# Residual add of a mixing block: beta added to x on GpSimd, scale and add in one VectorE step

## What is computed

```python
# 0: gated mixing over time
ctx    = ema(x);  gated = x * sigmoid([x, ctx] @ Wg.T + bg)
mod    = 0.5 + sigmoid(gelu(x @ Wn1.T + bn1) @ Wn2.T + bn2)          # 16 rows
temporal = sum_d softmax(blend)[d] * ema_d(gated * mod[d])           # 16 traces
out = (gelu(x @ Wsoma.T + bsoma) * sigmoid(temporal @ Wtemp.T + btemp)) @ Wout.T
x   = x + (out - mean(out)) / sqrt(var(out) + 1e-5) * gamma + beta
# 1: masked attention pooling
score = tanh(x @ W1 + b1) @ v;  x = x + softmax(masked score) @ x / count
# 2: 8 experts and a shared one, 256 -> 1024 -> 256
x = x + (1 - sg) * sum_e g[e] * (silu(x@Wg[e]) * (x@Wu[e])) @ Wd[e] + sg * shared(x)
# 3: head, 256 -> 1024 -> 256, part of W2 chosen per sequence
x = x + gelu(x @ W1 + b1) @ [W2, We[idx]] + [b2, be[idx]]
```

## Time and profile before

| | |
|---|---|
| median of 3 runs | 2799.22 us (2799.05 to 2800.12) |
| profiled execution | 2799.28 us |
| its span, first to last instruction | 2797.3 us |
| TensorE busy | 2765.7 us, 12786 matmuls |
| VectorE, ScalarE, GpSimd busy | 1796.6, 1456.9, 1219.6 us |
| granted TensorE clock | 0.999 of full |
| DMA | 232.48 MB, 83 GB/s |

### The profile page before, as it was taken

The page is one execution under the profiler, slowest core; times in us unless marked ns, Lnnn a source line. Parts: engine busy times, 40 slices in busy tenths (PEclk is TensorE's granted clock), DMA queues, the critical chain, the costliest instruction groups (busy, mean ns, idle before and its releaser), DMA issues.

```text
span 2797.3 us, 36734 instructions
## 1 busy us (share of the span) xinstructions
PE 2765.7 (99%) x12786; PEld 2294.8 (82%) x12786; DVE 1796.6 (64%) x2975; ACT 1456.9 (52%) x2649; POOL 1219.6 (44%) x954
## 2 busy tenths in 40 slices
PE   8899999999999999999999999999999999999999
PEld 5678888888878888888888888888888888888888
DVE  8899778767877666557755766555765563333443
ACT  4655656565447544555545644444644563333445
POOL 6266336533554355334543345433454333333334
PEclk9999999999999999999999999999999999999999
DMA  5344334433223222122321232211332131111221
GB/s 179 110 138 123 98 108 115 133 93 108 81 59 109 93 68 68 55 61 76 97 65 57 85 92 74 62 53 57 108 82 62 44 100 46 46 46 46 79 90 58
DMA packets 119607, 232.48 MB, mean 83 GB/s; under 512 B 13816, under 2 KB 61184, under 8 KB 119424
## 3 DMA queue, kind: packets, MB, share of 16 engines
q1 hardware_dynamic: 84144, 192.27, 22.4%
q10 hardware_dynamic: 32688, 29.47, 4.2%
q0 software_dynamic: 2592, 8.41, 0.9%
HBM read 221.98 MB, written 8.11 MB: 82 GB/s over the span
## 4 chain that ended last, share of the span: by engine, by line
PE 93%; DVE 5%; issue 1%; ACT 1%; DMA 0%; POOL 0%; DVEq 0%; SPq 0%; ACTq 0%
PE bank L625 20%; PE bank L626 20%; PE bank L627 20%; PE ps_out L625 10%; PE ps_out L627 10%; PE ps_out L626 10%; PE bank L618 1%; DVE trace L1263 1%; DVE trace L1349 1%; DVE w_lo L1474 1%; DVE hid L1509 0%; DVE trace L1423 0%; PE bank L660 0%; PE bank L646 0%; PE bank L651 0%
## 5 line engine op out<-in xcount | busy, mean ns | idle before, releaser
L1655 POOL TENSOR_TENSOR hid_lo<-hid,hid_hi 128x512 fp32r<-128x512 f32 x640 | 850.5, 1329 | 1528.2 <-ACT hid_hi L1192 1527.9
L625 PE MATMUL bank<-res_lo,w_hi 128*128 128x512 f32 x2428 | 955.1, 393 | 5.2 <-DVE hid L1509 4.3
L626 PE MATMUL bank<-res_hi,w_lo 128*128 128x512 f32 x2428 | 946.2, 390 | 0.0
L627 PE MATMUL bank<-res_hi,w_hi 128*128 128x512 f32 x2428 | 945.2, 389 | 0.0
L1509 DVE TENSOR_TENSOR hid<-hid,bank 128x512 f32<-128x512 f32 x576 | 394.2, 684 | 619.5 <-PE bank L627 592.0
L1161 ACT ACTIVATE hid<-bank 128x512 f32<-128x512 f32 x576 | 343.9, 597 | 586.7 <-PE bank L627 583.8
L1474 DVE TENSOR_TENSOR w_lo<-w_raw,w_hi 128x768 fp32r<-128x768 f32 (+2 forms) x520 | 497.6, 959 | 191.0 <-ACT w_hi L1122 148.9
L1122 ACT ACTIVATE w_hi<-w_raw 128x768 fp32r<-128x768 f32 x392 | 331.3, 845 | 480.7 <-PE ps_out L627 468.6
L625 PEld LDWEIGHTS bank<-res_lo,w_hi 128*128 128x128 f32 x2428 | 456.2, 188 | 98.0 <-DVE w_lo L1474 4.7
L627 PEld LDWEIGHTS bank<-res_hi,w_hi 128*128 128x128 f32 x2428 | 455.8, 188 | 96.8
L626 PEld LDWEIGHTS bank<-res_hi,w_lo 128*128 128x128 f32 x2428 | 456.2, 188 | 89.2
(11 more groups left out here) (226 smaller groups left out, 1599.7 us busy)
## 6 DMA issues: line engine op xcount, KB each, us to landing
w_raw<-in_chunks SPq DMA_DIRECT2D x392, 384.0 KB, 3.1
mod_on<-mod_rows ACTq DMA_DIRECT2D x154, 128.0 KB, 3.2
w_raw<-in_head_chunks SPq DMA_DIRECT2D x64, 224.0 KB, 2.5
stat<-mod_rows ACTq DMA_DIRECT2D x70, 128.0 KB, 3.1
x_in<-in_xT SPq DMA_DIRECT2D x16, 256.0 KB, 3.7
pre_x<-in_xT SPq DMA_DIRECT2D x14, 256.0 KB, 7.0
soma_rows<-pre_soma SPq DMA_DIRECT2D x14, 256.0 KB, 2.0
soma<-soma_rows SPq DMA_DIRECT2D x14, 256.0 KB, 3.5
```

The lines of the kernel that those rows point to most:

```text
L625: mm(out, wh, xl, start=start and i == 0, stop=False, skip_group_check=not lone)
L626: mm(out, wl, xh, start=False, stop=False, skip_group_check=not lone)
L627: last = mm(out, wh, xh, start=False, stop=end, skip_group_check=not lone)
L1655: nc.gpsimd.tensor_tensor(hid_lo[i % DEPTH][:], hid[i % 3][:], f(hid_hi[i % DEPTH][:]), ALU.subtract).then_inc(s_hlo, 1)
```

## The change

For blocks 1 to 7 piece 36 takes the form of block 0: GpSimd adds beta to x in place ahead of the seventh add (j = 15), and VectorE forms `x1` in two SCALAR_TENSOR_TENSOR, after a wait for GpSimd's stage "xb". The stage "affine" is gone, and the price of piece 36 in the planner goes from 1.4 to 1.0.

```diff
-    return {0: 1.3, 5: 1.0, 34: 1.7, 36: 1.4, 42: 1.5, 24: 0.0, 25: 0.0, 29: 0.0, 37: 0.0, 43: 0.0}.get(j, 0.7)
+    return {0: 1.3, 5: 1.0, 34: 1.7, 36: 1.0, 42: 1.5, 24: 0.0, 25: 0.0, 29: 0.0, 37: 0.0, 43: 0.0}.get(j, 0.7)
...
-            + ["t_lo", "prod", "p_lo", "q_lo", "rstd", "norm", "affine", "x1", "score",
+            + ["t_lo", "prod", "p_lo", "q_lo", "rstd", "norm", "x1", "score",
...
-SIDE_POOL = ((ADDED[:6] + ["xb"] + ADDED[6:], ADDED[:6] + ["xb"] + ADDED[6:-1]), ADDED)
+SIDE_POOL = ((ADDED[:6] + ["xb"] + ADDED[6:], ADDED[:6] + ["xb"] + ADDED[6:-1]), ADDED[:6] + ["xb"] + ADDED[6:])
...
                 elif j == 36:
+                    dve.wait_ge(l_pool[s], pool_at(s, b, "xb"))
                     mine("norm")
                     for h in range(DH):
-                        last = TS(cen[:, h, :], cen[:, h, :], gamma[:, h:h + 1], beta[:, h:h + 1], ALU.mult, ALU.add)
+                        last = STT(x1[:, h, :], cen[:, h, :], gamma[:, h:h + 1], X[:, h, :], ALU.mult, ALU.add)
                     last.then_inc(l_dve[s], 1)
-                    mine("affine")
-                    TT(x1[:], cen[:], X[:], ALU.add).then_inc(l_dve[s], 1)
...
-                    if b == 0 and d == 7:
-                        shift(s)
+                    if d == 7:
+                        shift(b, s)
...
-            def shift(s):
-
-                pool.wait_ge(l_dve[s], dve_at(s, 0, "gated"))
-                pool.wait_ge(l_pe[s], pe_at(s, 0, "soma"))
+            def shift(b, s):
+
+                X = x_in[s][b % 2]
+                pool.wait_ge(l_dve[s], dve_at(s, b, "gated"))
+                if b == 0:
+                    pool.wait_ge(l_pe[s], pe_at(s, 0, "soma"))
                 for h in range(DH):
-                    last = TS(x_in[s][0][:, h, :], x_in[s][0][:, h, :], beta[:, h:h + 1], None, ALU.add)
+                    last = TS(X[:, h, :], X[:, h, :], beta[:, h:h + 1], None, ALU.add)
                 last.then_inc(l_pool[s], 1)
```

## The result

| | before | after |
|---|---|---|
| median of the timed runs | 2800.11 us (16 runs, 2798.59 to 2803.65) | 2804.06 us (16 runs, 2802.26 to 2807.48) |
| ratio after/before | | 1.0015, 95% [1.0009, 1.0021] |
| profiled execution (span) | 2799.28 us (2797.3) | 2807.05 us (2804.8) |

The change costs about 4 us, 0.15%. It was forecast to gain 2.4. The difference stays under the 0.2% that I had named, a case that had 0.79, but the runs are enough to tell it from zero, the sign is the other one, and the time lies 2.6 us above the range.

A forecast was written before the change was run, and what follows sets the result against it. TensorE bounds the kernel, busy 2765.7 of 2797.3 us. The terms -0.95 + 1.5 - 1.6 - 2.4 + 1.0 = -2.45 us gave 2796.8 us, with a range of 2793.0 to 2801.5.

The forecast's parts named there:

- a case that had 0.79: The whole kernel's time stays within 0.2% of before, between 2793.6 and 2804.8 us; chance 0.79.
- Elsewhere the same dealing out can make new waits: Moved pieces at places not named make new TensorE waits: +1.0 us, bounds 0 and 6.4.
- lane 1's pieces 31 and 32: Four blocks: reciprocal a step later; square's low part shares its projection's step, VectorE sitting 2 to 3 us seven times.
- The two named moves: Trace piece behind the accumulation near 569 us, -1.60 us; exponentials a step earlier near 2266 us, -2.4 us.
- The residual in two steps: VectorE, blocks 1 to 7: 0.58 us saved 14 times; x1 waits near 302 and 836 us shrink, -0.95 us.
- The GpSimd pair: Added at 14 places, it delays VectorE; TensorE pays 0.75 us each near 239 and 774 us: +1.5 us.
- The reading of the earlier trace: At 145.91 us a w_lo took 3.64 us, about 0.93 plus GpSimd's add and hid_lo beside it.
- the cited rule: VectorE with two SBUF inputs and GpSimd take a shared port pair in turn, the first holding it a whole instruction.
- Rival 1: The GpSimd pair makes TensorE wait at most of the 14 places, 12.9 us, giving 2808.2 us; chance 0.07.
- Arithmetic as a whole: Shorter VectorE residual, -0.95 us, and the added GpSimd pair, +1.5 us, taken together.
- Rival 3: Moved pieces bring as much idle time as they remove: 2799 us, give or take 2; chance 0.27.
- Theory N: Set up for the experiments: something slows the first 110 us; first silu at 113.2 us in after, 110.3 before.

The follow-up runs named there:

- e2: Before with only the planner's price of piece 36 set to 1.0: old arithmetic, new order; 2805.12 us, +5.3 us against before.
- e8: e1 with three entries moved: trace piece near 569 us behind the accumulation, pieces 40 and 41 of block 7 a step earlier; 2796.60 us, -3.8 us against before.
- e1: After with the price of piece 36 left at 1.4: new arithmetic, old order; 2799.68 us, -0.2 us against before.
- e3: e1 with the GpSimd pair and VectorE's wait for it left out of blocks 1 to 7; 2799.40 us, -0.4 us against before.
- e5: After with the gather of the penalties issued three pieces later on GpSimd; 2801.31 us, +0.9 us against before.
- e10: e8 with GpSimd's four gathers of expert rows for blocks 0 and 1 put to steps 46 and 47; 2792.61 us, -8.2 us against before.
- e11: After with the price of piece 36 at 1.3, 43 entries differing from before; 2800.85 us, 0.0 us against before.
- e4: Before with the GpSimd pair added, VectorE still taking three instructions for the residual; 2801.44 us, +1.6 us against before.
- e7: After with pieces 25 and 26 of lane 1 put back a step in blocks 2, 3 and 7; 2803.71 us, +3.3 us against before.

## Why the prediction was wrong

- **The step that failed** is the term "Elsewhere the same dealing out can make new waits ... I take +1.0 us, one wait of middling size", with its bounds 0 and 6.4 us. e2 puts all moved pieces together at +5.3 us; with the two named gains taken off (-3.6, e8 less e1) the rest of the order costs about 8.9 us. Each of these differences to before has an error of some 2.5 us, so that this lies above the 6.4 is not certain; that it lies far above the 1.0 is. The trace of e2 shows 0.98 (324 us) + 2.4 (`one_lo`, three times) + 0.94 (835 us) + 0.96 (x1 near 584 us) + 0.92 (1342 us) = 6.2 us as new idle time; six new waits at about 0.2 us beside it make 7.4 (0.36 of the 0.96 is inside the -3.6 already, since e8 waits there too). Some 1.5 us stay unplaced, which is within that error.
- **Why it was set too low.** I bounded it by the size of the waits that were there before. But these were what is left when a list has been dealt out once; 231 entries dealt out anew are drawn from all collisions that can happen, and TensorE bears them only where there is slack. I looked at the places where a wait stood before and asked what became of it, and not at the entries that now fall beside a GpSimd run or ahead of a closing accumulation. The one mechanism that I named, lane 1's pieces 31 and 32, produced no wait of TensorE at all: VectorE sat there seven times as foreseen, 1.7 to 3.35 us each.
- **The two named moves** were right in mechanism and near in size, 3.6 us (e8 less e1) where I took 4.0. 1.60 near 569 went fully, but the trace piece now stands ahead of the residual, and TensorE waits for x1 instead, 0.36 before 579.85 in e8, which e1 does not have. Of 2.87 near 2268 the trace shows 1.20 left, so 1.67 gone where I took 2.4; together 3.27 of idle time, 2.9 with the new wait taken off. The rest may be TensorE's clock, which falls behind the long pauses near 2273 us in most profiles and never behind the short ones (last section).
- **The residual in two steps** was right: 473 ns, 28 times, x1 near 840 us at 1.41, in the old order 1.32 (e1; forecast 1.3), and the 0.36 near 302 us gone. A late x1 came at another place, 0.38 before 582.86, where the old form waits 0.96 (e2).
- **The GpSimd pair** was forecast at +1.5 us; the medians, 0.3 to 1.6, do not contradict it, but the traces show no cost in the old order (7.18 us of waits in e1, 7.45 in e3). The places were wrong: nothing near 239 and 774 us, where VectorE was fullest, but 0.78 us before 1341, where the accumulation that TensorE waits for came behind small `w_lo`. The reading of the earlier trace rows that stood behind the term was short: two gathers (0.97 at 143.56, 1.34 at 144.83) closed GpSimd's run up ahead of the add, and the cited rule, one instruction for each turn, does not give the wait for two that I said agreed with it. Rival 1 (the pair decides) had the right sign and the wrong cause; its 12.9 us did not come.
- **Arithmetic as a whole:** forecast -0.95 + 1.5 = +0.55 us; measured -0.2 us (e1), no difference.
- **Rival 3** (one wait for another) describes what happened; I gave it 0.27 and a spread of 2 us, which was too narrow. For waits of the moved pieces that pass the 0.2% line I had 0.01.
- **What is not explained by the change.** Of the 7.5 us between the two profiled spans, 2.9 lie before the first silu of the steps, where no instruction of block 0 changed. Theory N holds for the profile alone; the last section shows what it is. The medians differ by 4.

## What to carry to other kernels

A change in an instruction's assumed price, made beside a change in the instruction, is a change of its own: hold the order fixed, time the two apart, and then take from the new order only the entries that remove a wait that you can name. When a short VectorE instruction shows several times its own duration, look for a run of GpSimd instructions without a gap beside it, and for what closes its gaps, such as the issue of an indirect DMA; moving that away can be worth more than the arithmetic (3 us in e5, about 4 us in e10). The waits that a tuned order has left say nothing of those that another order will have.

## What the runs showed of the hardware

**An indirect DMA's issue on GpSimd closes the gaps of a run that holds VectorE.** The prediction gave it no price; in the kernel before each takes 0.94 to 1.51 us of GpSimd time, and what stands behind it starts later. A `w_lo` beside such an issue alone took its usual 0.95 us. Moving it changed a VectorE instruction from 3.43 to 0.88 us (e5) and from 3.64 to 0.93 us (e10).

**Which engine goes first can turn on little.** In after a `one_lo` started 0.34 us ahead of a `hid_lo`, beside a gather, and sat out the run (607.30 and 607.64). In e11 one started 0.35 us ahead of a `hid_lo`, beside a gather too (853.48 and 853.83), took its 0.69 us, and the `hid_lo` took 1.47 instead of 1.3. No run varied this alone.

**TensorE's clock falls for a few microseconds, in two parts of the program.** The stretch from 84 to 89 us has the same code in both kernels. Before and after (same columns as the stretches above):

```profile
84.00:89.00 5.00, 4.36 (x19) 3.49 (x20) 4.45 (x7) 3.60 (x7) 1.40 (x2) 1.00 0.19 54
```

```profile
84.00:89.00 5.00, 4.17 (x12) 3.43 (x13) 4.12 (x6) 2.73 (x5) 1.77 (x2) 0.66 0.20 54
```

In after the granted clock averages 0.66 there: part of the stretch ran at the lower of its two levels (1.2 of 2.4 GHz) and TensorE did 12 matmuls instead of 19. In e1 the clock falls behind two pauses of TensorE, 0.93 and 1.93 us; its timeline shows a matmul 128x512 every 0.43 us, and then 0.22 again:

```profile
2273.28 0.47 PE L625 MATMUL ps_out<-hid_lo,w_hi 128*128 128x512 f32 x1 [1.93 <-DVE acc L1531]
...
2275.84 0.63 PE L626 MATMUL bank<-res_hi,w_lo 128*128 128x512 f32 x1
2276.27 0.63 PE L627 MATMUL bank<-res_hi,w_hi 128*128 128x512 f32 x1
...
2277.47 0.39 PE L627 MATMUL bank<-res_hi,w_hi 128*128 128x512 f32 x1
2277.69 0.39 PE L625 MATMUL ps_out<-hid_lo,w_hi 128*128 128x512 f32 x1
```

In the 13 profiles the lower level shows only between 80 and 112 us and between 2270 and 2280 us. In the first part it comes and goes with code that does not differ: the granted clock from 90 to 112 us is 1.00 in five profiles, e4 and e7 among them, and 0.77 in e2 and e3, and the first silu starts between 108.7 us (e7) and 114.1 us (e3) accordingly. In the second part it goes with the pauses. Five kernels have the long ones of the earlier trace rows there (before, e1, e3, e4, e11); in four of them the granted clock from 2270 to 2280 us is 0.83, in the profile of before 1.00. The eight others have short ones, and all show 1.00. What it costs can be read from e1 and before: from the matmul behind the long pause to the start of the fifteenth after it, 4.41 us (2273.28 to 2277.69) against 2.88 us (2273.34 to 2276.22), 1.5 us. One profile of each kernel makes this likely and not certain; no run was made for it.

The scatter in the first part is of the size of this change's effect: a single pair of profiles can't rank these kernels. The medians of 10 to 33 runs of each, as taken here, have intervals of some 0.1% either way.
